# A mixture-of-experts layer: block results scattered straight to token order, and a final norm spread over three engines

## What is computed

```python
router_weights = softmax(xf @ rw + rb)
topw, topi = top_k(router_weights, 2); topw = softmax(topw)
combine = zeros((T, 8)).at[arange(T)[:, None], topi].add(topw)
h  = gelu(einsum('td,edf->etf', xf, w1) + b1)
eo = einsum('etf,efd->etd', h, w2) + b2
x  = layernorm(x + einsum('etd,te->td', eo, combine)) * ln3_g + ln3_b
```

## Time and profile before

| | us |
|---|---|
| median of 3 runs (3574.54 to 3578.53) | 3578.2 |
| the profiled execution, as timed | 3593.65 |
| its span, first to last instruction | 3591.9 |
| around the span | 1.75 |
| first instruction of the first block's transposes | 2871.28 |
| end of the last result copy | 3473.83 |

### The profile page before, as it was taken

How to read it: one execution, slowest core, us unless ns; L and a number is a source line. 1 busy time by engine, 2 the same in 40 slices (tenths; PEclk the granted TensorE clock), 3 DMA queues, 4 the chain that set the end, 5 groups by cost and what they waited for, 6 DMA issues and landing times. The chain is left out here.

```text
span 3591.9 us, 54697 instructions
## 1 busy us (share of the span) xinstructions
PE 3051.4 (85%) x18207; PEld 1719.0 (48%) x18207; DVE 2111.3 (59%) x4295; ACT 1893.7 (53%) x3859; POOL 1593.6 (44%) x2792
## 2 busy tenths in 40 slices
PE   6888999898899989899998989888885399999960
PEld 3435444443544454354444435443425177777850
DVE  4877887786788778678877867854352000000016
ACT  4665767567576766757675675735341032223210
POOL 5655554582565467257546725642301500000026
PEclk9999999999999999999999999988985599999985
DMA  3005221541422143042204313132303345455523
GB/s 86 16 27 109 57 65 30 115 95 30 99 61 54 30 92 71 28 83 58 56 28 92 70 29 84 40 75 54 55 9 116 134 147 170 159 171 172 175 73 114
DMA packets 270054, 290.11 MB, mean 81 GB/s; under 512 B 32056, under 2 KB 255680, under 8 KB 269808
## 3 DMA queue, kind: packets, MB, share of 16 engines
q1 hardware_dynamic: 261936, 270.21, 30.0%
q0 software_dynamic: 6144, 16.79, 1.4%
q10 hardware_dynamic: 1728, 0.01, 0.0%
HBM read 224.34 MB, written 62.39 MB: 80 GB/s over the span
## 5 line engine op out<-in xcount | busy, mean ns | idle before, releaser
L1250 ACT ACTIVATE probs<-ps,nbias,sc 128x512 f32<-128x512 f32 x1024 | 790.4, 778 | 275.5 <-DVE nbias L1131 216.9
L997 POOL TENSOR_SCALAR pq<-probs,rstep 128x512 f16<-128x512 f32 x1024 | 709.7, 693 | 252.0 <-PE ps L1364 168.4
L1148 DVE TENSOR_REDUCE m<-ps 128x1 f32<-128x512 f32 (+3 forms) x1024 | 561.1, 583 | 294.0 <-PE ps L1390 150.8
L1128 DVE TENSOR_REDUCE nmax<-ps 128x2 f32<-128x1024 f32 x512 | 620.8, 1212 | 95.4 <-PE ps L1356 94.8
L1387 PE MATMUL ps<-kst,qst 96*128 96x512 bf16 (+3 forms) x1024 | 331.4, 355 | 90.5 <-issue 50.7
L1140 DVE TENSOR_SCALAR big<-ps 128x1024 bf16<-128x1024 f16 x512 | 348.1, 680 | 63.1 <-PE ps L1364 61.4
L1364 PE MATMUL ps<-id,pq 128*128 128x128 f16 x4096 | 330.5, 226 | 47.5 <-DVE big L1140 41.3
L1875 DVE COPY yb<-moe_ps 128x256 f32<-128x256 f32 x78 | 33.1, 425 | 569.5 <-PE moe_ps L1725 569.5
L1409 PE MATMUL ps<-qst,kst 108*128 108x512 bf16 (+3 forms) x1024 | 306.3, 353 | 65.2 <-ACT big L1269 29.9
L1629 POOL DMA_INDIRECT got<-rows_out,slot_of x64 | 69.5, 1085 | 643.1 <-DMA rows_out<-yb 624.5
L1364 PEld LDWEIGHTS ps<-id,pq 128*128 128x128 f16 x4096 | 261.5, 101 | 192.1 <-issue 129.3
(11 more groups left out here) (205 smaller groups left out, 4621.7 us busy)
## 6 DMA issues: line engine op xcount, KB each, us to landing
e_w<-in_L_xattn_e_w_dram SPq DMA_DIRECT2D x78, 1024.0 KB
wring<-in_L_xattn_ff_w_dram SPq DMA_DIRECT2D x96, 256.0 KB, 2.9
parts<-parts_sb SPq DMA_DIRECT2D x64, 384.0 KB, 3.0
kst<-parts SPq DMA_DIRECT2D x192, 128.0 KB, 4.8
qst<-parts SPq DMA_DIRECT2D x192, 128.0 KB, 5.1
moe_in<-rows_in SPq DMA_DIRECT2D x39, 256.0 KB
rows_out<-yb SPq DMA_DIRECT2D x39, 256.0 KB, 2.2
rows_in<-zero SPq DMA_DIRECT2D x19, 512.0 KB, 4.0
```

Of the source, the lines that this page charges most:

```text
L997: nc.gpsimd.tensor_scalar(pq[:, u % 2, h, :], probs[:, u % 2, h, :], rstep[:, u % 2, h:h + 1], HALF_ROUND, ALU.mult, ALU.add).then_inc(SIG ...
L1128: nc.vector.tensor_reduce(nmax[:, n % 2, :], ps[:, a:a + 2, :], AX.X, ALU.max, negate=True).then_inc(SIG["M"], 1)
L1148: nc.vector.tensor_reduce(m32[:, g % 2, t, h:h + 1], bank(("A", B, s, n))[:, 0:width], AX.X, ALU.max, negate=True).then_inc(SIG["am"], 1)
L1250: nc.scalar.activation(probs[:, u % 2, h, :], ps[:, BANKS[("S", B, s, u)][h], :], ACT.Exp, bias=nbias[:, u % 2, h:h + 1], scale=sc[:, s:s ...
```

## The change

The rows that travel to the experts become 264 numbers long: each carries, behind its 256 features, eight integers, one for each expert, that say to which row of the result its copy goes (the token's number for its first expert, that plus 4096 for its second). They are computed on DVE (`goes_to`) and copied into `xs`. The filling rows carry an address out of bounds. For each half of a block DVE copies the column of the block's expert into `to`, and adds the expert's bias while it copies the result out of PSUM; `b2` is loaded into all 128 partitions for that. POOL then scatters each half to `rows_out`, now in token order, inside the block loop. SP's block store goes.

The bias sum, with its work on PE, ACT and DVE, goes, and with it `acc`, `comb` and PE's wait for them. The gathers go too: SP loads each chunk's two parts with two plain DMAs of 512 KB, four chunks ahead.

The final norm is laid out for a chunk as: DVE adds parts, takes the statistics and computes `shift`; ACT normalises; DVE applies the gain of the chunk before; POOL computes the reciprocal root, and adds the bias of the chunk before.

```diff
+ROW = D + NE
+TOKENS = NBATCH * N
...
-            nc.gpsimd.memset(zero[:, :], 0.0).then_inc(s_set, 1)
+            nc.gpsimd.memset(zero[:, 0:D], 0.0)
+            nc.gpsimd.memset(zero[:, D:ROW], 1.0).then_inc(s_set, 1)
...
+GOTS = 4
...
-        xs = sb("moe_x", [P, NTILES, D], F32)
-        acc = sb("acc", [P, NTILES, D], F32)
+        xs = sb("moe_x", [P, NTILES, ROW], F32)
...
-        b2 = sb("e_b2", [NE, D], F32)
+        b2 = sb("e_b2", [P, NE, D], F32)
...
-            sp.dma_start(b2[:, :], w["e_b2"]).then_inc(s_l, 16)
+            sp.dma_start(b2[:, :, :], w["e_b2"].rearrange("(a e) n -> a e n", a=1).broadcast_to([P, NE, D])).then_inc(s_l, 16)
             for c in range(NB):
-                sp.dma_start(xs[:, c * NT:(c + 1) * NT, :], mid[c].rearrange("(t p) d -> p t d", p=P)).then_inc(s_x[c], 16)
+                sp.dma_start(xs[:, c * NT:(c + 1) * NT, 0:D], mid[c].rearrange("(t p) d -> p t d", p=P)).then_inc(s_x[c], 16)
...
                     sp.wait_ge(yd, SUB * j + 3 * SUB)
                     if not isinstance(j, int):
                         sp.sem_inc(s_passed, 1)
-                    sp.dma_start(rows_out[bass.ds(j, 1)].rearrange("a (s p) d -> p a s d", p=P), yb[:, slot % 2, :, :].unsqueeze(1)).then_inc(s_ys[slot % 2], 16)
                     if exists(j + 2):
                         load_block(j + 2, slot % 2)
                     if exists(j + WSLOTS):
...
+            parts = rows_out.rearrange("(k c t p) d -> k c p t d", k=2, c=NB, p=P)
+
+            def load_parts(c):
+                for k in range(2):
+                    sp.dma_start(got[:, c % GOTS, k, :, :], parts[k, c]).then_inc(s_g[c % GOTS], 16)
+
+            for slot in range(2):
+                sp.wait_ge(s_ys[slot], 16 * SUB * ((BLOCKS + 1 - slot) // 2))
+            for c in range(GOTS):
+                load_parts(c)
+            for c in range(NB):
+                if c + GOTS < NB:
+                    sp.wait_ge(s_add, 2 * NT * (c + 1))
+                    load_parts(c + GOTS)
+                sp.wait_ge(s_y, c + 1)
+                sp.dma_start(out[c].rearrange("(t p) d -> p t d", p=P), y[:, c % 2, :, :]).then_inc(s_out[c % 2], 16)
...
+            def send_back(q, slot):
+                j = 2 * q + slot
+                for s in range(SUB):
+                    pool.wait_ge(yd, SUB * j + 2 * SUB + s + 1)
+                    if not isinstance(j, int):
+                        pool.sem_inc(s_passed, 1)
+                    nc.gpsimd.indirect_dma_start(rows_out, bass.IndirectOffsetOnAxis(ap=to[:, slot, s:s + 1], axis=0),
+                                                 yb[:, slot, s, :], None, bounds_check=2 * TOKENS - 1, oob_is_err=False).then_inc(s_ys[slot], 16)
+
+            with pool.Fori(0, BLOCKS // 2) as q:
+                for slot in range(2):
+                    send_back(q, slot)
+            if BLOCKS % 2:
+                send_back(BLOCKS // 2, 0)
+
+            for c in range(NB + 1):
+                if c < NB:
+                    i = c % 2
+                    pool.wait_ge(s_mv, NT * (c + 1))
+                    nc.gpsimd.tensor_tensor(ve[:, i, :], mv[:, i, :, 1], eps[:, :], ALU.add).then_inc(s_ve, 1)
+                    pool.wait_ge(s_ve, c + 1)
+                    if c >= 2:
+                        pool.wait_ge(s_nr, NT * (c - 1))
+                    nc.gpsimd.tensor_tensor(rstd[:, i, :], ve[:, i, :], minus_half[:, :], ALU.pow).then_inc(s_rs, 1)
+                if c:
+                    b = c - 1
+                    pool.wait_ge(s_ga, b + 1)
+                    if b >= 2:
+                        pool.wait_ge(s_out[b % 2], 16 * (b // 2))
+                    for t in range(NT):
+                        last = nc.gpsimd.tensor_tensor(y[:, b % 2, t, :], xs[:, b * NT + t, 0:D], bias[:, :], ALU.add)
+                    last.then_inc(s_y, 1)
...
-            for c in range(NB):
-                i = c % 2
-                if c >= 2:
...
-            for c in range(NB):
-                act.wait_ge(s_ct, c + 1)
...
+            for c in range(NB):
+                act.wait_ge(s_sh, c + 1)
+                for t in range(NT):
+                    x_t = xs[:, c * NT + t, 0:D]
+                    nc.scalar.activation(x_t, x_t, ACT.Identity, scale=rstd[:, c % 2, t:t + 1], bias=shift[:, c % 2, t:t + 1]).then_inc(s_nr, 1)
...
             then(last)
-            for k in range(2):
-                last = nc.vector.tensor_tensor(wq[:, k, :, :], eq[:, k, :, :], wide(wt[:, k, :]), ALU.mult)
-            then(last)
-            then(nc.vector.tensor_tensor(comb[:, :, :], wq[:, 0, :, :], wq[:, 1, :, :], ALU.add))
-            assert steps[0] == COMB_READY
             then(nc.vector.tensor_tensor(chosen[:, :, :], eq[:, 0, :, :], eq[:, 1, :, :], ALU.add))
+            assert steps[0] == CHOSEN_READY
+            then(nc.vector.scalar_tensor_tensor(out=goes_to[:, :, :], in0=eq[:, 1, :, :], scalar=float(TOKENS), in1=wide(token[:, :]),
+                                                op0=ALU.mult, op1=ALU.add))
+            then(nc.vector.tensor_copy(xs[:, :, :].bitcast(U32)[:, :, D:ROW], goes_to[:, :, :]))
+            assert steps[0] == DESTS_READY
...
-            for t in range(NTILES):
-                dve.wait_ge(s_bf, t + 1)
-                nc.vector.tensor_tensor(acc[:, t, :], ps[:, 2 + t % 2, 0:D], xs[:, t, :], ALU.add).then_inc(s_bd, 1)
+            for c in range(NB):
+                dve.wait_ge(s_x[c], 16)
...
-                dve.wait_ge(s_ys[slot], 16 * q + 16)
+                e = dve.value_load(owner[0:1, bass.ds(j, 1)], min_val=0, max_val=NE - 1)
+                if not isinstance(q, int) or q:
+                    dve.wait_ge(s_ys[slot], 16 * SUB * q)
                 for s in range(SUB):
                     dve.wait_ge(yf, SUB * j + s + 1)
-                    nc.vector.tensor_copy(yb[:, slot, s, :], ps[:, 2 + 2 * slot + s, 0:D]).then_inc(yd, 1)
...
+                    nc.vector.tensor_copy(to[:, slot, s:s + 1], xin[:, slot, s, :].bitcast(U32)[:, bass.ds(e + D, 1)])
+                    nc.vector.tensor_tensor(yb[:, slot, s, :], ps[:, 2 + 2 * slot + s, 0:D],
+                                            b2[:, bass.ds(e, 1), :].rearrange("p a n -> p (a n)"), ALU.add).then_inc(yd, 1)
+
+            for slot in range(2):
+                take_block(0, slot)
+            with dve.Fori(0, BLOCKS // 2 - 1) as q:
                 for slot in range(2):
-                    take_block(q, slot)
+                    take_block(q + 1, slot)
             if BLOCKS % 2:
                 take_block(BLOCKS // 2, 0)
...
+            def tile(c, t):
+                return xs[:, c * NT + t, 0:D]
+
+            for c in range(NB + 1):
+                if c < NB:
+                    dve.wait_ge(s_g[c % GOTS], 32 * (c // GOTS) + 32)
                     for k in range(2):
                         for t in range(NT):
...
+                            n = c * NT + t
                             if k:
                                 dve.wait_ge(s_add, c * 2 * NT + t + 1)
...
+                            nc.vector.scalar_tensor_tensor(out=tile(c, t), in0=got[:, c % GOTS, k, t, :], scalar=wt[:, k, n:n + 1],
+                                                           in1=tile(c, t), op0=ALU.mult, op1=ALU.add).then_inc(s_add, 1)
...
+                        dve.wait_ge(s_add, c * 2 * NT + NT + t + 1)
+                        nc.vector.bn_stats(bn6[:, c % 2, t, :], tile(c, t)).then_inc(s_st, 1)
...
                     for t in range(NT):
...
+                        dve.wait_ge(s_st, c * NT + t + 1)
+                        if c >= 2 and t == 0:
+                            dve.wait_ge(s_sh, c - 1)
+                        nc.vector.bn_aggr(mv[:, c % 2, t, :], bn6[:, c % 2, t, :]).then_inc(s_mv, 1)
+                if c:
+                    b = c - 1
+                    dve.wait_ge(s_nr, NT * (b + 1))
+                    a = xs[:, b * NT:(b + 1) * NT, 0:D]
+                    nc.vector.tensor_tensor(a, a, gain[:, :].unsqueeze(1).broadcast_to([P, NT, D]), ALU.mult).then_inc(s_ga, 1)
+                if c < NB:
+                    dve.wait_ge(s_rs, c + 1)
+                    if c >= 2:
+                        dve.wait_ge(s_nr, NT * (c - 1))
+                    nc.vector.scalar_tensor_tensor(out=shift[:, c % 2, :], in0=mv[:, c % 2, :, 0], scalar=-1.0, in1=rstd[:, c % 2, :],
+                                                   op0=ALU.mult, op1=ALU.mult).then_inc(s_sh, 1)
...
```

More of the change, by code:

```diff
@@ L1475, in experts @@
         wq = sb("wq", [P, 2, NTILES, NE], F32)
-        comb = sb("comb", [P, NTILES, NE], F32)
+        token = sb("token", [P, NTILES], F32)
+        goes_to = sb("goes_to", [P, NTILES, NE], F32)
         chosen = sb("chosen", [P, NTILES, NE], BF16)
@@ L1494, in experts @@
         yb = sb("yb", [P, 2, SUB, D], F32)
[L1495 to L1499, removed]
+        got = sb("got", [P, GOTS, 2, NT, D], F32)
+        bn6 = sb("moe_bn6", [P, 2, NT, 6], F32)
+        mv = sb("moe_mv", [P, 2, NT, 2], F32)
```

(25 more changed lines are left out.)

88 lines of the change are left out of this document (20 added, 68 removed).

## The result

| | before | changed |
|---|---|---|
| median of 4 runs each, us | 3578.36 (3574.54 to 3582.33) | 3550.99 (3547.51 to 3554.06) |
| ratio, 95% interval | | 0.992 [0.9905, 0.9935] |
| profiled execution, us | 3593.65 | 3552.56 |
| its span, us | 3591.9 | 3550.8 |

A forecast was written before the change was run, and what follows sets the result against it. PE, busy 85% of the span, was taken as the bound, leaving only the last 880 us to gain from. Timed: 3578.2 + 2.0 (head) + 0.1 (loop) - 20.5 (end) = 3559.8 us; range 3528 to 3572.

The forecast's parts named there:

- Profile against median: Waits beside the head's scatters: 15.3 us in the profiled run alone, so deleting the bias sum saves timed runs nothing.
- Head: Routing to first block: `b2` load costs 2.9 us, routing saves 0.9, scatters unchanged; 2.0 us later in timed runs.
- Loop: Block loop: scatters and block loads hidden under PE, DVE's extra work costing 0.1 us once, at the last block.
- the rival that ended slower: Block loop: scatters bring waits without cause to ACT's gelu, 94 us, about 3654; chance 0.06.
- Start of the end: Last result copy to first additions: SP loads at 3476.3, first additions at 3481.3 instead of 3488.17.
- A chunk: Final norm: 6.95 us undisturbed; with DVE and POOL blocking each other, chunk 1 8.8 and chunks 2 to 7 10.75.
- I take nearly the whole: Final norm: DVE and POOL wait out each other's instructions; each POOL bias addition delays DVE by 0.65 us.
- The drain: Last chunk: ACT 1.9, gain 1.3, POOL's additions 2.95, then 3.6 to the end; with hops 9.9 us.
- From there to the end 3.6: Last stretch, from POOL's last additions to the end of the span: 3.6 us.
- Together: The end, from first additions to end of span: finishes at 3571.4, 20.5 us earlier than 3591.9.
- The rival without interference: Final norm: DVE and POOL don't disturb each other, or hardly; the end 45.1 us earlier, 3535; chance 0.12.
- The rival of slow loads: The end: parts and output move at 180 GB/s, 70 us; within a remaining 0.04 for dearer head or loads, near 3575.

The follow-up runs named there:

- b2_late: The changed kernel with the load of `b2` issued behind the loads of `mid`, with its own semaphore; 3546.0 us, 0.9862.
- no_bias_sum: The kernel before without the bias sum, DVE filling `acc` from `xs` alone; ratio 1.0007, and 1.0017 when run again.
- shift_late: The changed kernel with `shift` of the previous chunk put between the two halves of a chunk's additions; 3536.93 us, 0.9847.
- no_pool_add: The changed kernel without the final bias additions on POOL, SP storing after the gain; 3538.31 us, 0.9891.
- old_norm: The changed kernel with the final norm of the kernel before, only the root on POOL and the rest on DVE; 3558.35 us, 0.9938.
- best1: The changed kernel with the edits of shift_late and b2_late together; 3533.75 us, 0.9835.
- weights_after: The kernel before with the first weight loads behind the scatters and the first blocks' rows; ratio 1.0022.

## Why the prediction was right in direction and short in size

**Profile against median** held. The 15.3 us of the earlier trace rows belonged to the profiled execution: two later profiles of the same kernel are without them, taking the bias sum away gains nothing, and the profiled span fell by 13.7 us more than the median (41.1 against 27.4).

**Head** was forecast at +2.0 and measured +2.7. "At the 359 GB/s at which `mid` arrives it costs 2.9 us" is 2.2 by `b2_late`; not foreseen were the 1.5 to 2 that the first load of `mid` takes besides, and their cause is open. The routing saves 1.2 (0.9 forecast): from the logits to the last result 20.2 us instead of 21.4. Rows of 1056 bytes cost the scatters nothing (85.8 against 85.9), as taken. PE's clock rose 7.1 us after the start of the first block (the three of before: 4.8, 6.2 and 6.6), and the first result copy came 16.9 us after that start instead of 16.2 to 16.4.

**Loop**: 0.1 forecast, 0.3 to 0.6 measured. It is the clock, as far as the profiles tell: `no_bias_sum`, which has nothing of the change in its loop and whose clock rose 7.4 us after the start, takes 602.8 as well, and `shift_late`, with a rise after 5.2, takes 602.1. Of 78 scatters none brought a wait without cause, so the rival that ended slower is refuted. Its assumption is weak too: of the four profiles that have the bias sum beside the 64 scatters of the head, one shows such waits.

**Start of the end**: 7.5 forecast from the last copy to the first additions, 8.6 measured. SP issues 3.0 after the copy instead of 2.4, and from there to the additions it is 5.6 (5.13 of it from issue to landing) instead of 5.0.

**A chunk** is the step that failed: "Chunk 1 is 8.8, and chunks 2 to 7 are 10.75". They are 7.7 and 9.23, and six times 1.52 is 9.1 us of gain that the forecast lacked. `no_pool_add` splits the 1.52. Without POOL's additions a chunk is 7.21, where my terms give 6.95 + 1.2 = 8.15: here 0.94 was too dear. DVE's own part from the additions to the end of the statistics is 4.85 where I took 5.33 from the last chunk of before: there DVE stood still for 0.15 us ahead of each of the two steps of the statistics, until the last result of the step before was there, and the changed kernel waits tile by tile. `shift` adds 0.08, not 0.2. And from the statistics to `shift` it is 2.28 with the gain between (3488.75 to 3491.03 in `no_pool_add`), 0.88 more than the 1.40, not 1.2. The mutual delay is 2.02 where I took 4 times 0.65: three POOL additions add 1.48 to the eight of DVE, 0.49 each. "I take nearly the whole" was thus a third too much. The kind of effect was right. By the Trainium skill, SBUF — State Buffer, "Who interferes with whom", the ports that DVE and GpSimd share are locked for the whole instruction; the rows agree that they exclude each other, in both directions (POOL's 0.20 becomes 1.09 behind a gain of 1.19), but the loser is not held by the full 0.72 of each POOL addition: the two runs of additions overlap and both become longer.

**The drain** was forecast at 9.9 from the last `shift` and is 12.9. The last gain and the last additions in the timeline of the changed kernel, then stretches (us, busy of PE, PEld, DVE, ACT, POOL, clock, DMA, GB/s):

```profile
3540.04 1.23 DVE L1930 TENSOR_TENSOR moe_x<-moe_x,gain 128x1024 f32<-128x1024 f32 x1 [2.14 <-ACT moe_x L1796]
3541.35 2.76 POOL L1674 TENSOR_TENSOR moe_y<-moe_x,bias 128x256 f32<-128x256 f32 x4 [1.42 <-DVE moe_x L1930]
```
```profile
3546.00:3547.00 1.00, 0.00 (x0) 0.00 (x0) 0.00 (x0) 0.00 (x0) 0.00 (x0) 0.50 0.57 200
3547.00:3548.00 1.00, 0.00 (x0) 0.00 (x0) 0.00 (x0) 0.00 (x0) 0.00 (x0) 0.50 0.00 0
```

The line with which the program ends, in the changed kernel and then in `old_norm` (duration in ns, start in us):

```profile
L1442 POOLq DRAIN  x1: 9260/9260/9260, 3541.3 to 3541.3; - x1
```
```profile
L1442 POOLq DRAIN  x1: 7512/7512/7512, 3548.0 to 3548.0; - x1
```

ACT, gain and POOL are as forecast. But the last store has landed by 3547, and the span ends at 3550.8; before, data moved until 3591 of 3591.9. "From there to the end 3.6" is 6.7 here. It is 3.4 in `old_norm`, which ends on DVE, and in `no_pool_add`, which also does, the data move into the last stretch; in `best1`, which ends on POOL, nothing moves in the last 4 us. The step that had it wrong is that the end hangs on the last store alone. It also hangs on POOL's closing instruction, DRAIN. It ends at 3550.57, 6.47 us after POOL's last addition (3544.11), and every engine's last instruction comes behind it. In all eight profiles of the changed kernel and its variants it ends 6.47 us after POOL's last work, in the six of before and its variants 5.33 us after it; why the two differ isn't known. In `old_norm` and in before, POOL's last work is a root (in `old_norm` until 3549.03, the DRAIN until 3555.50), so the DRAIN runs under DVE's work and the last store, and the store lands later (3555.90). In `no_pool_add` the two end within 0.1 us of each other. The changed kernel's last store has landed at 3547.04, so the DRAIN costs it 3.0 us. The last chunk's addition on DVE, which is idle there, would be the remedy; that wasn't tried.

**Together** the end came out 27.0 instead of 20.5: chunks 2 to 7 gave 9.1 more, chunks 0 and 1 1.6 more, the drain took back 3.0 and the start 1.1. The median moved by 8.8 more than forecast. These 6.5, less 0.7 of the head and 0.3 of the loop, are 5.5 of it; the rest lies in no stretch that was read. The chunks were too dear, the start and the drain too cheap, so that the total is nearer than its terms. The rival without interference (3535) fell: 2.0 us of every chunk are interference. The rival of slow loads fell too: no chunk waits for one.

## What to carry to other kernels

When one profile shows waits without a cause, set its own time against the median before pricing them: here they were 15 us of one execution and nothing of the others. Addresses carried in the rows let 78 scatters go under PE's work for 0.6 us at most and spared 64 gathers that nothing hid, which with some 4 us of finer waits is 25 of the 27 us, while the norm spread over a third engine brought 1.6 until DVE's one wait, for POOL's root, was put under other work (16 us). Between engines that exclude each other, add up each one's items against the period, and beside it what they take alone: in `shift_late` both engines fill the 6.82 us, but alone the items take 6.03 and 3.97. And look at what closes the program: an engine that works last may have a closing instruction behind its work, here 6.47 us on POOL.

## What was not expected of the hardware

- Of three executions of the same kernel that were profiled, one has ACT and DVE standing for up to 32.3 us with no releaser; nor did it come in `weights_after`, the only other kernel that has ACT and DVE at work there. Its cause stays open, and so does why before took 3592 in one of the comparisons, where it wasn't profiled; the changed kernel's variants beside it were no slower than elsewhere.
- PE's granted clock at the start of the stage (2.4 GHz at 1.00, 1.2 at 0.50) is not the same from one execution to the next, though PE is as busy. The stretch from 4 to 6 us after PE's start in the changed kernel, then in `best1` (columns as above, each engine's count in brackets):

```profile
2717.50:2719.50 2.00, 2.00 (x20) 2.00 (x20) 0.00 (x0) 0.41 (x2) 0.00 (x0) 1.00 1.10 359
```
```profile
2711.90:2713.90 2.00, 2.00 (x11) 2.00 (x11) 0.00 (x0) 0.23 (x1) 0.00 (x0) 0.50 1.10 358
```

  The one does 20 instructions in the 2 us, the other 11. The higher level lasted 3.4 us, and without it, transposes and logits needed 3.1 us more (40.4 instead of 37.3), in `no_bias_sum`, `no_pool_add`, `shift_late` and `best1`, but not in their neighbours: a scatter of 3 us in any single span.
- Two runs of additions on DVE and POOL don't simply queue. Four on POOL, 2.76 alone, take 3.14, 3.49 or 4.49, and the eight on DVE, 3.25 alone, take 4.73, 5.12 or 3.32. Single instructions show who gives way, but not why. The groups in a moment when each engine has one addition running, in the changed kernel (3491.9 to 3492.0) and in `shift_late` (3495.3 to 3495.4; x1 | busy us, mean ns):

```profile
L1916 DVE SCALAR_TENSOR_TENSOR moe_x<-got,wt,moe_x 128x256 f32<-128x256 f32 x1 | 1.0, 1019 | 0.0
```
```profile
L1674 POOL TENSOR_TENSOR moe_y<-moe_x,bias 128x256 f32<-128x256 f32 x1 | 2.2, 2235 | 0.0
```

  In the first DVE's addition is the long one (1.02 instead of 0.47) and POOL's has its 0.72; in the second POOL's takes 2.24 while four of DVE's pass at 0.47 each. DVE's addition is stamped 0.015 us ahead of POOL's in both cases, so the order of starts doesn't tell which one waits.
